# Half B's first round read by ScalarE into sums of its own, and layer 1's fp16 splits for turning replaced by fp32 products

## The reference, cut to what matters

```python
mask = (adj > 0.0).astype(x.dtype)
xj_proj = x @ W1a
diff = x[:, :, None, :] - x[:, None, :, :]
h = jax.nn.relu(xj_proj[:, :, None, :] + diff @ W1b + b1)     # 192 hidden
hm = jnp.einsum('bjkh,bjk->bjh', h, mask)
x = layernorm(x + hm @ W2 + deg[..., None] * b2)
```

## Time and profile before

| | us |
|---|---|
| median of 3 runs | 805.18 (803.99 to 805.34) |
| the profiled execution | 805.59 |
| its span, first to last instruction | 804.1 |
| VectorE busy | 762.4 (95%) |
| TensorE matmuls busy / weight loads | 695.8 (87%) / 568.7 (71%) |
| ScalarE busy | 640.9 (80%) |
| GpSimd busy | 549.3 (68%) |
| TensorE's granted clock, mean | 0.991 |

### The profile page before, as it was taken

The page is one execution under the profiler, slowest core; times in us unless marked ns, Lnnn a source line. Parts: engine busy times, 40 slices in busy tenths (PEclk is TensorE's granted clock), DMA queues, the critical chain, the costliest instruction groups (busy, mean ns, idle before and its releaser), DMA issues.

```text
span 804.1 us, 37406 instructions
## 1 busy us (share of the span) xinstructions
PE 695.8 (87%) x15984; PEld 568.7 (71%) x15984; DVE 762.4 (95%) x851; ACT 640.9 (80%) x1897; POOL 549.3 (68%) x625
## 2 busy tenths in 40 slices
PE   3768789889898989989899898989989898988885
PEld 2547677677787867768787777878677687867662
DVE  5799999999999999999999999999999999998983
ACT  5746676888888888888988888888988888887654
POOL 5534445677868677786867779696777969575772
PEclk9999999999999999999999999999999999999998
DMA  5533243233334323323323232433223243222000
GB/s 150 146 105 75 83 100 88 62 75 101 75 100 97 86 76 75 104 73 108 95 81 84 66 113 63 121 81 94 75 65 111 68 120 76 56 61 75 2 15 27
DMA packets 33316, 66.86 MB, mean 83 GB/s; under 512 B 5504, under 2 KB 6272, under 8 KB 33152
## 3 DMA queue, kind: packets, MB, share of 16 engines
q1 hardware_dynamic: 33152, 64.48, 30.3%
HBM read 22.52 MB, written 4.19 MB: 33 GB/s over the span
## 4 chain that ended last, share of the span: by engine, by line
issue 44%; PE 28%; DVE 21%; ACT 3%; DMA 2%; POOL 1%; SPq 0%; DVEq 0%; POOLq 0%
PE PS L649 20%; DVE AC L1196 11%; DVE AC L1217 7%; PE PS L903 3%; PE PS L968 2%; PE PS L723 2%; PE PS L886 1%; DMA VA<-VN 1%; DVE WM L1165 1%; ACT VN L1565 1%; DMA bs<-in_rows 1%; POOL MT L1780 0%; DVE AC L1212 0%; DVE DM L1175 0%; ACT YO L1484 0%
## 5 line engine op out<-in xcount | busy, mean ns | idle before, releaser
L1217 DVE SCALAR_TENSOR_TENSOR AC<-PS,AC 128x1152 f32<-128x1152 f32 (+4 forms) x288 | 333.2, 1157 | 11.6 <-PE PS L649 10.7
L1196 DVE SCALAR_TENSOR_TENSOR AC<-PS,AC 128x1152 f32<-128x1152 f32 (+4 forms) x256 | 291.0, 1137 | 1.6 <-PE PS L903 1.3
L649 PE MATMUL PS<-DM,VA 128*64 128x192 fp8e5 (+1 forms) x2048 | 126.4, 244 | 41.4 <-DVE AC L1196 29.5
L649 PEld LDWEIGHTS PS<-DM,VA 128*64 128x64 f16 x2048 | 81.3, 110 | 77.8 <-DVE AC L1196 49.6
L649 PE MATMUL PS<-DM,VB 128*64 128x192 fp8e5 (+1 forms) x2048 | 123.9, 240 | 0.7 <-DVE AC L1212 0.2
L903 PE MATMUL PS<-DM,VB 128*64 128x192 fp8e5 (+1 forms) x1024 | 85.9, 245 | 23.7 <-DVE AC L1217 19.2
L1175 DVE TENSOR_SCALAR DM<-CW 128x1536 uint16<-128x1536 uint16 (+1 forms) x132 | 96.2, 750 | 1.0 <-DMA CW<-WM 1.0
L649 PEld LDWEIGHTS PS<-DM,VB 128*64 128x64 f16 x2048 | 89.5, 110 | 2.6 <-DVE AC L1217 1.5
L1812 POOL TENSOR_TENSOR XE<-XQ,XT 128x512 f16<-128x512 f32 x32 | 41.3, 1289 | 70.2 <-ACT XT L1552 70.2
L1838 POOL TENSOR_TENSOR AC<-AC,SD 128x512 f32<-128x512 f32 (+1 forms) x62 | 65.3, 1063 | 29.4 <-DVE DM L1175 29.4
L903 PEld LDWEIGHTS PS<-DM,VB 128*64 128x64 f16 x1024 | 45.6, 108 | 54.1 <-DVE AC L1217 26.9
(11 more groups left out here) (240 smaller groups left out, 2067.5 us busy)
## 6 DMA issues: line engine op xcount, KB each, us to landing
CW<-WM SPq DMA_DIRECT2D x128, 160.0 KB, 2.8
XQ<-in_xq SPq DMA_DIRECT2D x32, 256.0 KB, 2.7
VA<-VN SPq DMA_DIRECT2D x64, 128.0 KB, 2.3
VB<-VN SPq DMA_DIRECT2D x64, 128.0 KB, 2.3
AT<-in_adjt SPq DMA_DIRECT2D x15, 512.0 KB, 4.6
...
```

Of the source, the lines that this page charges most:

```text
L649: last = e.matmul(o[k], lhs[:, k], rhs, **flags)
L1196: e.scalar_tensor_tensor(t, tiles(PS[:, b + p:b + 3, :])[:, :, cols], 0.0, t, ALU.max, ALU.add).then_inc(s["sx"], 1)
L1217: e.scalar_tensor_tensor(t, tiles(PS[:, r, :])[:, :, cols], 0.0, t, ALU.max, ALU.add).then_inc(s["sy"], 1)
```

## The change

**Half B's round 1.** ScalarE gets `round_b(q, 1)`: one relu from PSUM into a tile of its own, BB[q % 2], three pieces in the last tile. VectorE starts with round 2 and adds into BB. `clear` is gone. The sums of A and B now meet in SD: `add_a` adds AC's middle to SD, `add_b` adds BB's middle, both on GpSimd (in the last tile `add_b` is VectorE's, as `add_u` was). `out0_a` and `out0_b` read SD. In the diff below, the first hunk is VectorE's, then come `round_b`, `round_a` and `seeds` of ScalarE, then GpSimd's. AC, BB, VN, VA and VB have rows of 192 columns instead of 256.

```diff
@@ VectorE
         def round_b(q, n):
+                if n == 1:
+                    return
                 b = 3 * (q % 2)
-                if n == 1:
-                    ve.wait_ge(s["clr"], q + 1)
-                    ve.wait_ge(s["sx"], 9 * q + 9)
-                dst = tiles(AC[q % 3][:])[:, :, cols]
+                dst = BB[q % 2][:, :, cols.start - 64:cols.stop - 64]
@@ ScalarE
+            def round_b(q, n):
+                if n > 1:
+                    return
+                b, dst = 3 * (q % 2), BB[q % 2][:]
+                ac.wait_ge(s["ad"], 2 * (q - 1))
+                ac.wait_ge(s["sov"], q - 1)
...
+                ac.wait_ge(s["gy"], 9 * q + 1)
+                t, r = (dst[:, tile[2]], slice(b + 1, b + 2)) if q == NQ - 1 else (dst, slice(b, b + 3))
+                e.activation(t, tiles(PS[:, r, :])[:, :, back], ACT.Relu).then_inc(s["sy"], 1)
...
             def round_a(q, n):
-                ac.wait_ge(s["o0"], q - 2)
+                ac.wait_ge(s["aa"], 2 * (q - 2))
             def seeds(q):
-                ac.wait_ge(s["ad"], 2 * (q - 2))
+                ac.wait_ge(s["o0"], q - 2)
@@ GpSimd
-            def clear(q):
-                po.wait_ge(s["o0"], q - 2)
-                e.memset(tiles(AC[q % 3][:])[:, :, 192:256], 0.0).then_inc(s["clr"], 1)
+            def add_a(q, k):
+                po.wait_ge(s["im"], 2 * q + k + 1)
+                po.wait_ge(s["sx"], 9 * q + 9)
+                e.tensor_tensor(u, u, AC[q % 3][:, h, nat], ALU.add).then_inc(s["aa"], 1)
+            def add_b(q, k):
+                    po.wait_ge(s["aa"], 2 * q + k + 1)
                     po.wait_ge(s["sy"], 9 * q + 9)
+                    e.tensor_tensor(u, u, BB[q % 2][:, h, 0:128], ALU.add).then_inc(s["ad"], 1)
```

**Turning in fp32.** `split_x1` and `split_h` are gone on both engines, and TensorE takes X1 and GT as they are:

```diff
-                    if main_unit:
-                        both(o, SQ[:, k:k + 2, :].rearrange("p a n -> p (a n)"), idh[:], start=True, stop=False)
-                        last = both(o, X1l[:, k:k + 2, :].rearrange("p a n -> p (a n)"), idh[:], start=False, stop=True)
+                    if s is main and not late(u):
+                        last = both(o, X1[:, k:k + 2, :].rearrange("p a n -> p (a n)"), ident, start=True, stop=True)
...
-                        both(o, SYf[:, n], BDH[:], start=True, stop=False)
-                        last = both(o, GTl[:, n], BDH[:], start=False, stop=True)
+                    last = both(o, GT[:, n], BDC[:], start=True, stop=True)
```

**New tables.** All six are replaced:

```diff
 ORDER = (
-    ("s2b", "pp3", "bp", "", "pe", "trprbd", "", "t", "te", "tpb", "pr", "epeee", "d", "pe", "", "pc", "d", "", "e0r1"),
-    ("sp", "dp", "2b3b", "dt", "p", "bt", "t", "et", "pr", "dlendpn", "", "pdd", "dp", "dcn", "pddb", "p", "pd", "0pd1", "r"),
+    ("s", "eb2b", "t3peb", "r", "p", "rp", "t", "td", "etp", "ree", "ee", "ppd", "p", "bpp", "bepd", "b", "d", "0", "e1r"),
+    ("sb", "2", "bp3db", "t", "p", "lp", "p", "ptttb", "ppb", "dnrpn", "d", "dbe", "ed", "dpn", "", "dpd", "dr", "p", "d01"),
 )
```

More of the change, by code:

```diff
@@ L263, in build @@
         DM = [sb(f"DM{i}", [128, 2, 768], U16) for i in range(RD)]
-        AC = [sb(f"AC{i}", [128, 3, 512]) for i in range(3)]
+        AC = [sb(f"AC{i}", [128, 6, H]) for i in range(3)]
+        BB = [sb(f"BB{i}", [128, 6, H]) for i in range(2)]
         SO = sb("SO", [128, 4, F])
@@ L516, in parts_of_u @@
                     if t > 1:
-                        do("add_u", t - 2, k)
+                        do("add_b", t - 2, k)
+                    yield
+                for k in range(2):
+                    if t:
+                        do("add_a", t - 1, k)
                     yield
@@ L751, in yt @@
                 g, c, w, p = unit(u)
-                main_unit = s is main and not late(u)
                 pe.wait_ge(s["h"], u + 1)
-                if main_unit:
-                    pe.wait_ge(s["hl"], u + 1)
                 for name, v in gates:
@@ L1846, in soon @@
                 hints.append((e, e.mark_branch_hint_location()))
[L1848 removed]
+            follow(main_order, {"soon": soon, "setup": setup, "parts": parts, "count": count, "x_split": x_split, "split_x": split_x, "mask": mask, "split_xg": split_xg, "split_ms": split_ms, "s_ov": s_ov, "scale_u": scale_u, "add_a": add_a, "add_b": add_b, "dgen": dgen, **gpsimd_layer1(e, po, s)})
         def gpsimd_dense(e):
```

119 lines of the change are left out of this document (47 added, 72 removed), and 2 rows, old and new, of the table MAIN.

## The result

The median is 799.77 us (798.63 to 800.82, 5 runs) against 805.03 us (803.99 to 805.34, 5 runs) in the same session: a ratio of 0.9935, interval 0.9922 to 0.9947. The change gains 5.3 us where 14.0 were forecast. The profiled execution took 798.63 us with a span of 794.2; before it was 805.59 and 804.1.

A forecast was written before the change was run, and what follows sets the result against it. VectorE was taken to pace the kernel. Boundary gains of 0.65 + 0.25 = 0.9 us per pair over 15.5 pairs make 14.0 us, other terms 0: 805.6 - 14.0 = 791.6 us, range 770 to 808.

The forecast's parts named there:

- the chain at the boundary: Where tiles meet: seeds, TensorE and ScalarE's round 1 reads set when round 2 of B, then of A, can start.
- the pair's gain: Every two tiles in the steady part: 0.9 us gained, over 15.5 pairs 14.0 us.
- First tile and end: Start and last tile of the kernel: no work leaves the chain there, 0 us.
- 1.5 us around the span: Time outside the profiled span: 1.5 us, included in the 805.6 us from which the gain is subtracted.
- from round 2 on each round pair costs VectorE what it cost before: Rest of each tile behind the boundary: VectorE's cost unchanged, so only the two boundary stretches can shorten.
- an early SD: Boundary into even tiles: if the seeds' read ends as early as 2.6 us, A2 starts at 6.6, 0.5 us gained.
- The split between the boundaries: Gain per pair by boundary: middles of 0.65 us into odd tiles and 0.25 us into even ones.
- Rival 3: ScalarE's in-order queue from B1 to the next SD becomes the bound: 47.54 us per pair, kernel 820.6 us; chance 0.17.
- Turning at nothing: TensorE, middle of the tile: fp32 turning of features and state adds 0.8 us per pair, 12 us in all, costed 0.
- room in TensorE's round: One turning block beside one round is 1.6 us, against VectorE's 1.27 plus 1.27 that TensorE may run ahead: 0.
- the 11 us that GpSimd is idle: GpSimd's idle time in a pair: covers its extra 1.1 us per pair, costed at nothing unless state `h` is late.
- Contention of `dgen`: Boundary shifts on VectorE beside GpSimd additions: 1.8 us could come back, taken as 0 because longer shifts fill idle time.

The follow-up runs named there:

- experiment 4: The changed kernel with half B's round 1 read by VectorE at boundaries into odd tiles only, by ScalarE into even ones: 800.4 us, ratio 0.9938.
- first order of experiment 10: The changed kernel with the last tile's steps between rounds 1 and 2 of half B spread over later gaps: 799.72 us, ratio 0.9937.
- Experiment 11: The changed kernel with 34, 66 or 130 unused one-column writes ahead of VectorE's first instruction: 799.12, 797.63 and 798.77 us.

## Why the prediction was right and wrong

In short: the chain at the boundary was right, and the pair's gain nearly so. The step that failed is the part of the sum that was put at nothing: "First tile and end: no work leaves the chain there, 0", which cost 3.1 us, and the 1.5 us around the span, taken to stay, which became 4.4. A third failed without much harm to the number: "from round 2 on each round pair costs VectorE what it cost before".

**The steady pair: right, 0.9 forecast, 0.77 measured.** The chain of the boundary came out within 0.6 us everywhere: SD into odd ended at 3.44 (3.59 forecast), B2 at 5.67 (5.9) and A2 at 7.10 (7.35); into even 5.26 (5.8) and 6.53 (7.07, or 6.6 with an early SD). ScalarE's idle time is 4.6 us (4.5 forecast), VectorE's share 92% (91%), its waits 24.5 us ahead of B (30 to 40 forecast). VectorE was ahead by 13.0 us at B9 of tile 30 (760.98 against 748.01), nearly the whole 14.0, but that is partly luck. The first round 9 comes 0.5 us later than before (61.58 against 61.12); the next four tiles gain 3.1 us and the last one 1.7, where 0.45 a tile makes 2.3; the 25 between gain 8.6 where 11.3 were forecast.

**The split between the boundaries: the sizes met, the place didn't last.** 0.64 at the odd boundary fits the 0.65 forecast. But 0.6 of it is lost in the same tile, partly at the wait ahead of A4: the 16.31 us from A2 on, in place of 15.72, are what the forecast took as unchanged. That ScalarE's read gained nothing there (experiment 4) was not foreseen. The even boundary gives 0.57 where 0.25 was taken. So that 0.77 came near 0.9 is luck in part: the two boundaries gave 1.21 us, and the rest of the pair took 0.44 back. Rival 3's reading of the queue was half right: ScalarE's in-order row from the scaling to the seeds bounds the odd boundary, but as a chain through SD, not as a shortage of time.

**"First tile and end: 0" failed: 3.1 us.** From B9 of tile 30 to the end after needs 46.2 us, before 43.1. The forecast had taken no row of that stretch, and so did not see that ahead of round 2 VectorE would idle 5.12 us in one wait. The first order of experiment 10 shortens that wait (2.77 us ahead of round 2) and gains nothing at the end, so what sets the end stays open.

**"1.5 us around the span" failed: 2.9 us.** The profiled runs had 1.5 and 4.4. Experiment 11 shows what it hangs on: removing 34 VectorE instructions, and their waits, moved the end of its program, and with 66 writes more the tail is 1.3 to 1.6 us again. 13.0 - 3.1 - 2.9 = 7.0 us is the difference of the two profiled executions (805.59 - 798.63); that the medians differ by 5.3 is the spread of the runs, of which the profiled one of after is the fastest.

**Turning at nothing: wrong in both directions.** Alone it costs 4.1 us, and in after's tables its absence costs 59.5 (859.27 - 799.77). The argument (room in TensorE's round) missed the in-order queues behind the product, and "the 11 us that GpSimd is idle" missed that its work ahead of the state comes in one row. Neither the new tables alone nor ScalarE's read alone was run, nor the narrower VN, so their own shares are not known.

**Contention of `dgen`: rightly taken as 0.** Two shifts beside GpSimd's addition took 2.09 us, two behind it 1.01 (experiment 4), and B2 started at the same distance. By the Trainium skill (GPSIMD Engine Reference, Specifications) GpSimd and VectorE contend for shared SBUF interfaces. The rows agree (2.09 against 1.01 us), and show that here the loss fills a hole.

A further loss has no cause yet: single stalls of TensorE that the profile calls "issue", 1.6 us above the steady periods in after (tiles with 22.58, 22.62, 23.86 and 24.17 us) against 0.2 in before, somewhat different in each run of the new kernels.
